# Layer norm 2 interleaved with mix 1's keys and values, by groups of four tiles

## The reference, cut to what matters

```
xn = layernorm(x)                      # layer 0: GNN + linear attention, then a mixture of experts
x = x + gnn0(xn, ...) + mix0(xn, ...)
x = x + ffn0(layernorm(x), ...)
xn = layernorm(x)                      # this is "layer norm 2" (k == 2 in the kernel)
x = x + gcn(xn, ...) + mix1(xn, ...)
x = x + ffn1(layernorm(x), ...)

def mix1(x, w_qkv, w_out, b_out):      # 8 heads of 64
    q, k, v = split(x @ w_qkv.T)
    k, v = instance_norm(k), instance_norm(v)
    dots = einsum('bhnd,bhne->bhde', k, v)
    out = einsum('bhnd,bhde->bhne', q, dots) / N
    return out @ w_out.T + b_out
```

## Time and profile before

| what | value |
|---|---|
| time, median of 3 runs | 2373.67 us (2372.1 to 2376.24) |
| time of the profiled execution | 2379.11 us |
| its span from the first to the last instruction | 2377.5 us |
| PE busy | 2129.0 us (90%) |
| DVE busy | 1726.1 us (73%) |
| ACT busy | 1207.3 us (51%) |
| mean granted TensorE clock | 0.928 |

### The profile page before, as it was taken

The page is one execution under the profiler, slowest core; times in us unless marked ns, Lnnn a source line. Parts: engine busy times, 40 slices in busy tenths (PEclk is TensorE's granted clock), DMA queues, the critical chain, the costliest instruction groups (busy, mean ns, idle before and its releaser), DMA issues. The chain is left out here.

```text
span 2377.5 us, 46528 instructions
## 1 busy us (share of the span) xinstructions
PE 2129.0 (90%) x17787; PEld 1962.6 (83%) x17787; DVE 1726.1 (73%) x3488; ACT 1207.3 (51%) x2817; POOL 463.3 (19%) x389
## 2 busy tenths in 40 slices
PE   4496999999964999999599999999997999999997
PEld 2355999999953999999377899989996999999996
DVE  5838878877567887887566655565556887888885
ACT  3324555555441776766452544454444325666774
POOL 2750000000004334444000000000000032444443
PEclk9756999999965999999699999999997999999998
DMA  6111333333442799787200466646652005787785
GB/s 197 51 37 51 112 85 92 106 85 105 132 146 87 227 190 265 232 232 231 62 1 24 117 194 190 178 117 191 189 159 94 19 30 178 223 226 227 227 229 165
DMA packets 237322, 338.85 MB, mean 143 GB/s; under 512 B 29721, under 2 KB 198758, under 8 KB 236966
## 3 DMA queue, kind: packets, MB, share of 16 engines
q1 hardware_dynamic: 208800, 296.14, 40.0%
q0 software_dynamic: 24848, 35.68, 9.1%
q10 hardware_dynamic: 3446, 3.97, 0.5%
HBM read 258.83 MB, written 76.90 MB: 141 GB/s over the span
## 5 line engine op out<-in xcount | busy, mean ns | idle before, releaser
L2145 PE MATMUL bank<-WB_r,XN_r 128*128 128x448 f32 x1400 | 399.7, 367 | 3.7 <-DVE WB_r L2104 3.7
L2104 DVE TENSOR_TENSOR WB_r<-WB,WB_r 128x448 fp32r<-128x448 f32 x350 | 213.9, 624 | 166.2 <-ACT WB_r L2097 166.1
L2097 ACT CAST WB_r<-WB 128x448 fp32r<-128x448 f32 x350 | 197.6, 568 | 222.2 <-PE bank L2145 216.5
L1280 POOL TENSOR_TENSOR XN_r<-XN,XN_r 128x320 fp32r<-128x320 f32 x20 | 20.6, 1029 | 1370.0 <-DVE XN L1411 1370.0
L2145 PEld LDWEIGHTS bank<-WB_r,XN_r 128*128 128x128 f32 x1400 | 263.2, 188 | 26.8 <-DVE wb__r L2070 4.4
L1702 PE MATMUL bank<-SC_r,WB_r 128*128 128x256 f32 (+1 forms) x2064 | 256.0, 284 | 15.9 <-issue 13.8
L1702 PEld LDWEIGHTS bank<-SC_r,WB_r 128*128 128x128 f32 x2064 | 250.0, 192 | 20.3 <-issue 20.3
L915 ACT CAST WB_r<-bank 128x200 fp32r<-128x200 f32 x391 | 137.7, 352 | 200.5 <-PE bank L899 198.8
L1717 PE MATMUL bank<-R_r,H_r 128*128 128x256 f32 x1752 | 219.1, 285 | 13.2 <-DVEq L1489 9.3
L1717 PEld LDWEIGHTS bank<-R_r,H_r 128*128 128x128 f32 x1752 | 212.9, 192 | 13.7 <-issue 9.0
L1566 ACT ACTIVATE wb_<-bank,WB 128x256 f32<-128x256 f32 (+1 forms) x344 | 133.6, 477 | 98.1 <-issue 63.7
(11 more groups left out here) (373 smaller groups left out, 5306.6 us busy)
## 6 DMA issues: line engine op xcount, KB each, us to landing
WB<-adjw SPq DMA_DIRECT2D x350, 224.0 KB, 2.8
WB<-in_f_pack SPq DMA_DIRECT2D x127, 512.0 KB
WB<-in_f_pack SPq DMA_DIRECT2D x62, 640.0 KB
adjw<-X SPq DMA_DIRECT2D x24, 1600.0 KB, 7.5
WB<-in_f_pack SPq DMA_DIRECT2D x65, 516.0 KB
xd<-XN SPq DMA_DIRECT2D x15, 640.0 KB
y<-X SPq DMA_DIRECT2D x10, 640.0 KB, 3.3
X<-y SPq DMA_DIRECT2D x10, 640.0 KB, 7.1
```

The lines of the kernel that those rows point to most:

```text
L2097: e.copy(split_w(m)[0], RAW[m % PR]).then_inc(S("whigh"), 1)
L2104: e.tensor_tensor(al, RAW[m % PR], ah.bitcast(F32), ALU.subtract).then_inc(S("wlow"), 1)
L2145: mm_ = e.matmul(conv_bank(k, band, c)[:, 0:PW], x[st][:, o], y, start=(st == 0 and i == 0), stop=(st == T - 1 and i == 2))
```

## The change

Layer norm 2 and the forming of the keys and values become one loop over the groups. On each engine the order is now: the norm of group g, then the copies (and splits) of group g-1, then the keys and values of the tiles of group g-1. The norm functions for one group are cut out of the old loops (`norm_group_dve`, `norm_group_act`) and used by the other layer norms as before. The casting of the weights stands ahead of all this, where before it stood behind the norm.

As the stages now overlap, PSUM is divided: the transposes of layer norm 2 take B[0] and B[1] (each used again by the next group), the keys B[2], B[3] and B[6], the values B[4] and B[5], the dots B[7]. The low part xtl moves from XN's memory, which is now still being written, to four buffers in WB.

```
+    def turn_bank(k, g, c):
+        return B[c] if k == 2 else B[(2 * g + c) % 4]
+
     def turn_pe(e, k, g):
         ts = tiles_of(g)
         for c in range(2):
-            bk = B[(2 * g + c) % 4]
-            if g >= 2:
+            bk = turn_bank(k, g, c)
+            if k == 2 and g:
+                e.wait_ge(S(f"xt{c}"), G * k + g)
+            elif g >= 2:
                 e.wait_ge(S(f"xt{c}"), G * k + g - 1)
...
-    xth, xtl = (v.rearrange("p (c n) -> p c n", c=2) for v in (hr_[:, :], XNr[:, :]))
+    xth = hr_[:, :].rearrange("p (c n) -> p c n", c=2)
+    xtl = [WBr[:, i * 1024:(i + 1) * 1024].rearrange("p (c n) -> p c n", c=2) for i in range(4)]
...
     def key_bank(t):
-        return B[t % 4]
+        return B[(2, 3, 6)[t % 3]]
 
     def value_bank(t):
-        return B[4 + t % 3]
+        return B[4 + t % 2]
...
     def mix1_act(e):
...
         e.wait_ge(S("centred"), 2)
         for c in range(2):
             e.copy(kvh[:, c], wkv[:, c]).then_inc(S("high1"), 1)
...
+        for g in range(G + 1):
+            if g < G:
+                norm_group_act(e, 2, g)
+            if g:
+                turn_act(e, 2, g - 1)
+                split_act(e, g - 1)
+                for t in tiles_of(g - 1):
+                    values_act(e, t)
+        for t in (T, T + 1):
+            values_act(e, t)
...
     def mix1_dve(e, c):
         for i in range(2):
             e.wait_ge(S("high1"), 0 + i + 1)
             e.tensor_tensor(kvl[:, i], wkv[:, i], kvh[:, i].bitcast(F32), ALU.subtract).then_inc(S("low1"), 1)
...
+        ready = x_back(e)
+        for g in range(G + 1):
+            if g < G:
+                norm_group_dve(e, 2, g, ready)
+            if g:
+                turn_dve(e, 2, g - 1)
+                split_dve(e, g - 1)
+                for t in tiles_of(g - 1):
+                    keys_of_dve(e, c, t)
+        for t in (T, T + 1):
+            keys_of_dve(e, c, t)
...
     def mix1_pe(e):
...
+        for g in range(G + 1):
+            if g < G:
+                turn_pe(e, 2, g)
+            if g:
+                for t in tiles_of(g - 1):
+                    values_pe(e, t)
+        for t in range(T, T + 3):
+            values_pe(e, t)
...
@@ -2209,7 +2252,6 @@
...
-        norm_act(e, 2)
         mix1_act(e)
@@ -2248,7 +2290,6 @@
...
-        norm_dve(e, 2, x_back(e))
         mix1_dve(e, c)
@@ -2276,7 +2317,6 @@
...
-        norm_pe(e, 2)
         mix1_pe(e)
```

More of the change, by code:

```diff
@@ L438, in statistics_dve, with norm_group_dve @@
         e.wait_ge(S("norm"), n + 2 * len(ts))
+    def norm_group_dve(e, k, g, ready):
+        ts, i = tiles_of(g), G * k + g + 1
+        o = slice(ts[0], ts[-1] + 1)
+        statistics_dve(e, k, g, ready)
+        e.tensor_scalar(rstd[:, o], mv[:, o, 1], 1.0, 1e-5, ALU.mult, ALU.add).then_inc(S("var"), 1)
+        e.wait_ge(S("std"), i)
+        e.reciprocal(rstd[:, o], rstd[:, o]).then_inc(S("norm"), 1)
+        e.wait_ge(S("norm"), normed(k, g))
+        e.scalar_tensor_tensor(nbias[:, o], mv[:, o, 0], -1.0, rstd[:, o], ALU.mult, ALU.mult).then_inc(S("nb"), 1)
     def norm_dve(e, k, ready):
         for g in range(G):
[L442 to L449, removed]
+            norm_group_dve(e, k, g, ready)
             if g:
@@ L452, in norm_dve, with norm_group_act @@
         turn_dve(e, k, G - 1)
+    def norm_group_act(e, k, g):
+        ts, i = tiles_of(g), G * k + g + 1
+        o = slice(ts[0], ts[-1] + 1)
+        e.wait_ge(S("var"), i)
+        e.sqrt(rstd[:, o], rstd[:, o]).then_inc(S("std"), 1)
+        e.wait_ge(S("nb"), i)
+        for t in ts:
+            e.activation(XN[:, t, :], X[:, t, :], ACT.Identity, scale=rstd[:, t:t + 1],
+                         bias=nbias[:, t:t + 1]).then_inc(S("xn"), 1)
     def norm_act(e, k):
         for g in range(G):
[L456 to L463, removed]
+            norm_group_act(e, k, g)
             if g:
@@ L482, in turn_act @@
         e.wait_ge(S("xT"), 2 * (G * k + g) + 1)
-        e.copy(XT[:, 0, ts[0] * 128:(ts[-1] + 1) * 128], B[2 * g % 4][:, 0:len(ts) * 128]).then_inc(S("xt0"), 1)
+        e.copy(XT[:, 0, ts[0] * 128:(ts[-1] + 1) * 128], turn_bank(k, g, 0)[:, 0:len(ts) * 128]).then_inc(S("xt0"), 1)
     def turn_dve(e, k, g):
@@ L487, in turn_dve @@
         e.wait_ge(S("xT"), 2 * (G * k + g) + 2)
-        e.tensor_copy(XT[:, 1, ts[0] * 128:(ts[-1] + 1) * 128], B[(2 * g + 1) % 4][:, 0:len(ts) * 128]).then_inc(S("xt1"), 1)
+        e.tensor_copy(XT[:, 1, ts[0] * 128:(ts[-1] + 1) * 128], turn_bank(k, g, 1)[:, 0:len(ts) * 128]).then_inc(S("xt1"), 1)
     def scores_pe(e, k, g):
@@ L1891, in key_bank, with split_act, values_act @@
     def key_bank(t):
-        return B[t % 4]
+        return B[(2, 3, 6)[t % 3]]
     def value_bank(t):
-        return B[4 + t % 3]
+        return B[4 + t % 2]
     def cols_of(g):
         return slice(g * 512, min((g + 1) * 512, NP))
-    def mix1_act(e):
[L1901 to L1906, removed]
+    def split_act(e, g):
+        e.wait_ge(S("xt1"), 2 * G + g + 1)
+        e.wait_ge(S("xt0"), 2 * G + g + 1)
+        for c in range(2):
+            e.copy(xth[:, c, cols_of(g)], XT[:, c, cols_of(g)]).then_inc(S("high1"), 1)
+    def values_act(e, t):
+        if t >= 2:
+            _, g8 = norms_of(t - 2)
+            e.wait_ge(S("kvnorm"), t - 1)
+            e.sqrt(g8, g8).then_inc(S("kvroot"), 1)
+        if t >= T:
+            return
+        sq = sqbuf[t % 2]
+        if t >= 2:
+            e.wait_ge(S("kvsum"), t - 1)
+        for c2, bk in enumerate((key_bank(t), value_bank(t))):
+            e.wait_ge(S("kvm"), 2 * t + c2 + 1)
+            e.activation(sq[:, c2 * 512:(c2 + 1) * 512], bk, ACT.Square).then_inc(S("kvsq"), 1)
+        if t >= 4:
+            e.wait_ge(S("dots"), t - 3)
+        e.copy(kvbuf[t % 4][:, 512:1024], value_bank(t)).then_inc(S("vals"), 1)
+    def mix1_act(e):
         e.wait_ge(S("centred"), 2)
@@ L1910, in mix1_act @@
             e.copy(kvh[:, c], wkv[:, c]).then_inc(S("high1"), 1)
[L1911 to L1930, removed]
@@ L1932, in mix1_dve @@
-    def mix1_dve(e, c):
[L1933 to L1937, removed]
+        for g in range(G + 1):
[6 more added lines that the diff above has]
+                    values_act(e, t)
@@ new lines, in mix1_act, with split_dve, keys_of_dve @@
+        for t in (T, T + 1):
+            values_act(e, t)
+    def split_dve(e, g):
+        if g >= 4:
+            e.wait_ge(S("kvm"), 8 * (g - 3))
+        n = cols_of(g).stop - cols_of(g).start
+        for k in range(2):
+            e.wait_ge(S("high1"), 2 + 2 * g + k + 1)
+            e.tensor_tensor(xtl[g % 4][:, k, 0:n], XT[:, k, cols_of(g)], xth[:, k, cols_of(g)].bitcast(F32),
+                            ALU.subtract).then_inc(S("low1"), 1)
+    def keys_of_dve(e, c, t):
+        if t >= 2:
+            _, g8 = norms_of(t - 2)
+            e.wait_ge(S("kvroot"), t - 1)
+            c.add(e.reciprocal(g8, g8))
+            if t >= 6:
+                e.wait_ge(S("dots"), t - 5)
+            c.wait()
+            e.tensor_tensor(kvbuf[(t - 2) % 4][:, 0:512].rearrange("p (g d) -> p g d", d=64),
+                            key_bank(t - 2).rearrange("p (g d) -> p g d", d=64),
+                            g8.unsqueeze(2).to_broadcast([128, 8, 64]), ALU.mult).then_inc(S("keys"), 1)
+        if t >= T:
+            return
+        v16, g8 = norms_of(t)
+        if t >= 4:
+            e.wait_ge(S("keys"), t - 3)
+        e.wait_ge(S("kvsq"), 2 * t + 2)
+        e.tensor_reduce(v16, sqbuf[t % 2].rearrange("p (g d) -> p g d", d=64), AX, ALU.add).then_inc(S("kvsum"), 1)
+        e.wait_ge(S("kvsum"), t + 1)
+        c.add(e.tensor_scalar(v16, v16, 1.0 / 64, 1e-5, ALU.mult, ALU.add))
+        c.wait()
+        e.tensor_tensor(g8, v16[:, 0:8], v16[:, 8:16], ALU.mult).then_inc(S("kvnorm"), 1)
@@ L1980, in mix1_dve @@
             e.tensor_tensor(X[:, t, :], X[:, t, :], bout1, ALU.add).then_inc(S("mixed_dve"), 1)
-    def mix1_pe(e):
[L1983 to L2007, removed]
@@ new lines, in values_pe @@
+    def values_pe(e, t):
+        if t >= 3:
+            r, kb_ = rows_of(t - 3), kvbuf[(t - 3) % 4]
+            e.wait_ge(S("keys"), t - 2)
+            for j in range(4):
+                m = e.matmul(dt4[:, j, :], kb_[0:r, 512 + j * 128:512 + (j + 1) * 128], kb_[0:r, j * 128:(j + 1) * 128],
+                             start=(t == 3 and j == 0), stop=(t == T + 2), skip_group_check=True)
+            m.then_inc(S("dots"), 1)
+        if t >= T:
+            return
+        if t % 4 == 0:
+            e.wait_ge(S("low1"), 2 + 2 * (t // 4) + 2)
+        for c2, bk in enumerate((key_bank(t), value_bank(t))):
+            if c2 == 0 and t >= 3:
+                e.wait_ge(S("keys"), t - 2)
+            if c2 == 1 and t >= 2:
+                e.wait_ge(S("vals"), t - 1)
+            for c in range(2):
+                high = xth[:, c, t * 128:(t + 1) * 128]
+                low = xtl[t // 4 % 4][:, c, t % 4 * 128:(t % 4 + 1) * 128]
```

(4 more changed lines are left out.)

## The result

| | before | changed |
|---|---|---|
| time, median | 2373.68 us (4 runs, 2372.1 to 2376.24) | 2407.31 us (4 runs, 2404.71 to 2408.15) |
| ratio | | 1.0135, 95% interval 1.0114 to 1.0157 |
| span of the profiled execution | 2377.5 us | 2406.6 us |
| mean granted clock | 0.928 | 0.922 |
| from the first statistics of layer norm 2 to the masking of the dots | 1145.74 to 1276.42: 130.7 us | 1140.02 to 1303.10: 163.1 us |

The change made the kernel slower, by 33.6 us on the medians; 35.0 was forecast, and 2407.31 stands against 2408.7. In the two profiled executions the stage grew by 32.4 us. The spans differ by 29.1 only, since the stage begins 5.7 us earlier in the profile of the changed kernel and what follows it takes 2.4 us longer.

A forecast was written before the change was run, and what follows sets the result against it. PE was taken to set the pace of the keys and values, after a norm in which it does only transposes. Boundaries +52.8, earlier start -18.5, tail +0.7: +35.0 us on 2373.7, so 2408.7 us, range 2392 to 2415.

The forecast's parts named there:

- What starts earlier: Start of the stage: weights' casts become free and PE starts tile 0 at 1155.5 instead of 1173.98, 18.5 us earlier.
- The full boundary: Between groups, norm of groups 2 to 5, four times: PE waits for the norm; 26.4 us a group, 105.6 in all.
- E: The time at which the last tile of a group ends on PE; boundary times are counted from it.
- The dots at half clock: Dots behind a full boundary's transposes: between 0.81 and 1.6 us, taken as 1.6.
- The clock's return: Head of each group after PE's idle time: 3.8 us at half clock from the first key matmul, losing 1.9 us.
- the short one: Boundary with the norm of group 6, one tile: tile t ends at E + 11.8, the group takes 22.9 us.
- the rule that I weighed: At the boundaries, half clock counted from the transposes: loss 0.4 us per full boundary, 0.85 in the short one; sum +28.
- my row: Profile row of the old norm: PE busy 2.58 of 3 us with transposes, clock 0.50; so transposes weren't counted toward the return.
- The last boundary and the tail: No norm: tile 24 starts at about E + 3.5; the 8.7 us from there to the masking stay, plus 0.7 for the clock.
- The banks: PSUM division in the key and value tiles: three key banks cost nothing, two value banks are copied over 4 us early.
- the clock held: Rival at the group boundaries: clock holds or returns at once, +20.0 us, 2393.7; chance 14% with what lies between.
- The faster rival: Rival at the boundaries: norm hides under the matmuls, PE loses only its transposes, -13.5 us, 2360; chance 5%.

The follow-up runs named there:

- the one with the banks alone: Kernel before in its old order, with the changed kernel's division of PSUM and its waits; ratio 1.0002, stage 135.3 us against 130.7.
- the kernel with the copies first: Changed kernel with copies and split of group g-1 ahead of group g's norm, transposes behind a group's first tile; ratio 1.006 to before.
- the extra matmuls: Changed kernel plus 28 unused 128x512 matmuls on PE at each of five boundaries with a norm; ratios to before 1.0081 and, again, 1.0094.
- the spread kernel: Changed kernel's work and banks, with norm, copies and splits cut into pieces in slots between tiles; ratio 0.991 to before, stage 111.9 us.
- one piece between tiles: Spread kernel with a group's whole norm as one piece, in the slot four tiles ahead; ratio 1.0 to before, stage 132.1 us.

## Why the prediction was right

The forecast had the sign, the mechanism and the size; 33.6 us were measured and 35.0 forecast. That the total is so near is in part luck: the long stretch from tile 3's end to tile 24's start was forecast 4.8 us too long (132.0 against 127.2), and the tail behind it 2.6 us too short. By its steps:

- **What starts earlier.** Forecast: the first key matmul 9.8 us after the first statistics. Measured: 9.8 (1140.02 to 1149.84).
- **The full boundary.** Forecast from E: statistics at 2.3, ACT's copy from 6.84 to 7.4, split ready at 9.45, the next group's first matmul at 10.5. Measured at the first one: 2.2, 6.8 to 7.3, 9.35, 10.7. The gaps of PE for the copy are 7.37, 7.44, 7.45 and 7.44 us. The experiment that moves the norm behind the copies, the one that spreads it and the one with the banks alone show that the order is the cause, and not only that the times agree.
- **The dots at half clock.** Taken at 1.6; 1.57 here (1173.01 to 1174.58).
- **The clock's return is the term that was off.** I charged 3.8 us at half from the first key matmul of each group, a loss of 1.9, and a period of 26.4 us for a group. The windows over transposes and dots, and then over the first tile, for three of the boundaries, say less:

```profile
1171.20:1174.60 3.40, 3.36 (x17) 3.36 (x17) 2.10 (x4) 1.25 (x3) 0.00 (x0) 0.50 0.00 0
1174.60:1178.30 3.70, 3.70 (x16) 3.00 (x16) 0.00 (x0) 0.60 (x1) 0.00 (x0) 0.81 0.02 4
1196.70:1200.00 3.30, 3.24 (x17) 3.24 (x17) 2.10 (x4) 1.26 (x4) 0.00 (x0) 0.51 0.00 0
1200.00:1202.90 2.90, 2.90 (x16) 2.36 (x15) 0.00 (x0) 0.60 (x1) 0.00 (x0) 1.00 0.00 0
1221.50:1224.90 3.40, 3.36 (x17) 3.37 (x17) 2.10 (x4) 1.25 (x3) 0.00 (x0) 0.50 0.00 0
1224.90:1228.80 3.90, 3.90 (x14) 3.11 (x14) 0.00 (x0) 0.60 (x1) 0.00 (x0) 0.70 0.00 0
```

The first tile of a group took 3.5 us (1174.58 to the next dots at 1178.11), 2.9 and 3.9 at these three, 3.0 at the fourth and 4.2 at the short one, against 2.9 at full clock: a loss of 0.7, 0, 1.1, 0.1 and 1.4 and not 1.9. The transposes of the full boundaries follow each other at 25.5, 24.8 and 25.9 us. At the five boundaries the clock was back 3.2 to 5.7 us after the first transpose. In the kernel with the copies first, whose tiles start with no transposes ahead, it was back 3.1 to 5.1 us after the first key matmul. So the 3.8 us should have begun at the transposes. I had kept them out because of the norm's stretch of before, where transposes with gaps stayed at half clock; no run has transposes without gaps and without dots behind them, so what those alone would do is open. Here the rule that I weighed, of the Trainium skill (TensorE: Matmul & The Clock Gate, Part 1: The HAM clock gate), that sustained activity brings the full clock, was nearer than my row. For the stretch from tile 3 to tile 24 the count from the transposes gives 125.0 us and mine 132.0, and 127.2 were measured; its sum, +28, is further from the 32.4 of the stage than mine only by the tail.
- **The last boundary and the tail** cost more than charged, which made up for some of that: tile 24 began 3.6 us behind tile 23, where 3.5 was forecast, but ran mostly at half clock, as did the last dots (4.08 us where they took 2.24). From tile 24's start to the masking are 12.0 us, in both profiles of the changed kernel, where I had 9.4. The kernel with the copies first has the same gap of 2.66 us ahead of tile 24 but took only 8.7 us from there to the masking (1279.38 to 1288.06), with the last dots at 2.24. So the gap alone doesn't make it, and what does is open.
- **The banks** at nothing: right between the tiles. In the norm they cost 2.4 us when it runs by itself, which I had not looked at; in the changed kernel, where most of the norm stands behind a longer chain, they show only in the second group's transposes.
- **The rivals.** In the changed kernel the clock held at no boundary without the extra matmuls; with them the changed kernel's loss is +19 to +22, next to the +20.0 that I gave this case. The faster rival, the norm hidden under the matmuls, did not come to be in this order; it is what the spread kernel does, with another: -18.7 us in the stage.

The early start (18.4 us) and the loss at the boundaries don't cancel, and this is why: in the old order the norm of a group took 3.3 us on average (six groups from 1145.74 to 1165.74), since its parts overlap with those of its neighbours. At a boundary it holds PE for 7.4 us, since ACT and DVE wait for each other and PE for both.

## What to carry to other kernels

Putting two stages into one loop did not by itself overlap them here, on engines that take their instructions in order. What counted was whether a piece stood at a place where its engine would wait anyhow, and whether it was about as short as that wait. Look in the timeline for the wait of the follower engines in each step (1.15 us here), cut the second stage's work to that size, give each piece a step's distance from the one that feeds it, and the critical engine pays only for its own part. Of the four places tried, behind the last link of a group's chain was the dearest (+1.35%; copies first +0.6%, one piece between tiles 0.0%, spread -0.9%), and it was paid twice, since the idle time of PE also halved its clock.

## What was unexpected of the hardware

- PE did useless work for 6.7 us at each boundary and the kernel became 11 us faster: the granted clock was 1.00 from 1160 to 1290 us, and transposes and dots took 2.0 us instead of 3.3.
- A wait of 2.44 us ahead of the last dots, the same in all ten profiles, is followed in six of them by dots at full clock or nearly so (2.24 to 2.30 us), in one by 3.16 us, and in three by dots at half (4.08 us): both profiles of the changed kernel and that of the banks alone. An idle time ahead of tile 24 doesn't settle it: the kernel with the copies first has one as well, and 2.24; the one with the banks alone has none, and 4.08. What settles it is open; it is worth 1.8 us here.
